# Attention with unnormalised probabilities: the reciprocal row sums multiply each unit's output on VectorE, spread over the partitions through DRAM

## The reference, cut to what matters

```python
scores = jnp.einsum('bqhgd,bkhd->bhgqk', q, k) * scale
bias = jnp.where(rel >= 0, -slopes * sqrt_dist, -jnp.inf)
attn = jax.nn.softmax(scores + bias[None], axis=-1)
out = jnp.einsum('bhgqk,bkhd->bqhgd', attn, v).reshape(B, S, NH * D)
return out @ w_o
```

## Time and profile before

| | |
|---|---|
| median of 3 runs | 2512.18 us (2511.98 to 2513.4) |
| time of the profiled execution | 2510.83 us |
| its span | 2508.5 us, mean granted clock 0.986 |
| PE busy | 2413.6 us (96%) |
| PEld busy | 2049.7 us (82%) |
| DVE busy | 1503.8 us (60%) |
| ACT busy | 1382.8 us (55%) |
| POOL busy | 779.4 us (31%) |
| DMA | 455.93 MB, mean 182 GB/s |
| chain that ended last | PE 87%, ACT 5%, DVE 4%, DMA 2% |

### The profile page before, as it was taken

The page is one execution under the profiler, slowest core; times in us unless marked ns, Lnnn a source line. Parts: engine busy times, 40 slices in busy tenths (PEclk is TensorE's granted clock), DMA queues, the critical chain, the costliest instruction groups (busy, mean ns, idle before and its releaser), DMA issues.

```text
span 2508.5 us, 35023 instructions
## 1 busy us (share of the span) xinstructions
PE 2413.6 (96%) x12128; PEld 2049.7 (82%) x12128; DVE 1503.8 (60%) x2817; ACT 1382.8 (55%) x3075; POOL 779.4 (31%) x1029
## 2 busy tenths in 40 slices
PE   5999999997899999999799999999999999999999
PEld 4787888886778888888688888888888888888887
DVE  6657455565755555545566666666656666666664
ACT  4432133334534123333777777777777777777764
POOL 3211000000320100000334535446345364454634
PEclk8999999998999999999999999999999999999999
DMA  4536344545345544543755565655656556555543
GB/s 148 189 132 213 134 161 158 201 174 218 115 135 185 176 151 168 201 169 141 279 193 188 184 214 182 219 175 182 220 188 218 185 183 212 195 201 201 185 168 126
DMA packets 118319, 455.93 MB, mean 182 GB/s; under 512 B 11945, under 2 KB 12089, under 8 KB 109184
## 3 DMA queue, kind: packets, MB, share of 16 engines
q1 hardware_dynamic: 86176, 334.37, 38.6%
q0 software_dynamic: 31968, 119.33, 13.7%
HBM read 276.96 MB, written 176.69 MB: 181 GB/s over the span
## 4 chain that ended last, share of the span: by engine, by line
PE 87%; ACT 5%; DVE 4%; DMA 2%; issue 1%; POOL 1%; SPq 0%; DVEq 0%; ACTq 0%; POOLq 0%
PE ps L637 27%; PE ps L639 27%; PE ps L638 27%; PE ps L824 5%; ACT wo L886 1%; ACT probs L1026 1%; DVE stats L1135 1%; ACT pt_hi L886 1%; DMA q<-qk_s 1%; ACT rows L915 1%; ACT probs L1040 1%; DVE w_lo L1121 0%; ACT res_hi L886 0%; DMA lora_lo<-lora_s 0%; DVE pt_lo L1121 0%
## 5 line engine op out<-in xcount | busy, mean ns | idle before, releaser
L886 ACT ACTIVATE w_hi<-raw 128x1024 fp32r<-128x1024 f32 x196 | 207.0, 1059 | 559.3 <-PE ps L639 440.3
L1121 DVE TENSOR_TENSOR w_lo<-raw,w_hi 128x1024 fp32r<-128x1024 f32 x196 | 239.1, 1224 | 357.8 <-ACT w_hi L886 357.6
L1389 DVE TENSOR_TENSOR acc<-ps,acc 128x512 f32<-128x512 f32 x448 | 298.3, 687 | 249.5 <-issue 225.1
L637 PE MATMUL ps<-x_hi,w_hi 128*128 128x512 f32 x1120 | 436.2, 389 | 0.0
L639 PE MATMUL ps<-x_hi,w_lo 128*128 128x512 f32 x1120 | 435.8, 389 | 0.0
L638 PE MATMUL ps<-x_lo,w_hi 128*128 128x512 f32 x1120 | 435.7, 389 | 0.0
L637 PE MATMUL ps<-wo,op_hi 128*128 128x512 f32 x896 | 365.5, 408 | 24.1 <-DVE wo L1121 24.1
L1026 ACT ACTIVATE probs<-probs,neg_max 128x512 f32<-128x512 f32 (+3 forms) x512 | 284.2, 567 | 172.2 <-DVE neg_max L1358 172.2
L639 PE MATMUL ps<-wo,op_lo 128*128 128x512 f32 x896 | 355.3, 397 | 0.0
L638 PE MATMUL ps<-wo,op_hi 128*128 128x512 f32 x896 | 354.4, 396 | 0.0
L1358 DVE CUSTOM_DVE_ANT_0 probs<-ps,bias 128x512 f32<-128x512 f32 (+3 forms) x512 | 220.7, 487 | 111.4 <-PE ps L639 107.5
(11 more groups left out here) (155 smaller groups left out, 4700.6 us busy)
## 6 DMA issues: line engine op xcount, KB each, us to landing
raw<-w_all SPq DMA_DIRECT2D x70, 1024.0 KB, 5.3
q<-qk_s SPq DMA_DIRECT2D x128, 512.0 KB, 3.9
acc<-acc_s SPq DMA_DIRECT2D x128, 512.0 KB, 5.2
acc_s<-acc SPq DMA_DIRECT2D x112, 512.0 KB, 7.8
qk_s<-res_hi POOLq DMA_DIRECT2D x40, 1024.0 KB, 4.6
qk_s<-res_a POOLq DMA_DIRECT2D x20, 1024.0 KB, 9.1
qk_s<-res_b POOLq DMA_DIRECT2D x20, 1024.0 KB, 5.2
k<-qk_s SPq DMA_DIRECT2D x32, 512.0 KB, 3.6
```

The source lines that it names most:

```text
L637: pe.matmul(to, st_hi, mv_hi, start=start, stop=False, skip_group_check=True)
L886: nc.scalar.activation(to, source, ACT.Copy).then_inc(signal, 1)
L1121: nc.vector.tensor_tensor(to, source, high.bitcast(F32), ALU.subtract).then_inc(signal, 1)
L1389: nc.vector.tensor_tensor(to, fill[f % 2][:, :], to, ALU.add).then_inc(s_acc, 1)
```

## The change

The four ACT instructions of `normalise` are gone and the transposes wait for the exponentials instead. ACT's copy `outputs` is gone; DVE now reads ps_o, multiplies by the reciprocal row sums and writes at_raw. There, the query rows lie along the free axis and are the same for all partitions, so a unit's 512 reciprocals have to stand in every partition: SP writes them to DRAM, waits for that DMA, and reads them back broadcast. In the tables, weight step 4 has its high part one place earlier, and its low part is made by POOL in four pieces instead of by DVE. Some small tensors are moved in SBUF to make room.

```diff
-HIGHS_FIRST = {10: (4, 6)}
-HIGHS_LAST = {8: (0, 1), 9: (3, 2), 10: (5,)}
+HIGHS_FIRST = {10: (6,)}
+HIGHS_LAST = {8: (0, 1), 9: (3, 2, 4), 10: (5,)}
 LOWS_EARLY = {9: (0,), 10: (2,)}
-LOWS_MIDDLE = {9: (1,), 10: (4,)}
-LOWS_LAST = {9: (3,), 10: (6, 5)}
+LOWS_MIDDLE = {9: (1,), 10: (6,)}
+LOWS_LAST = {9: (3,), 10: (5,)}
+BY_DVE = (0, 1, 3, 2, 6, 5)
+LOWS_POOL = {10: (4,)}
+BY_POOL = (4,)
...
+            def spread(n):                       # SP
+                if not 0 <= n < UNITS:
+                    return
+                sp.wait_ge(s_inv, n + 1)
+                if n >= 2:
+                    sp.wait_ge(s_at_raw, n - 1)
+                sp.dma_start(inv_s[n % 2].rearrange("(p i) -> p i", i=QT), row_inv[:, n % 2, :]).then_inc(s_inv_s, 16)
+                sp.wait_ge(s_inv_s, 16 * (n + 1))
+                if n == 0:
+                    sp.wait_ge(s_bank, 4 * TOTAL)
+                sp.dma_start(inv_all[n % 2][:, :], inv_s[n % 2].partition_broadcast(P)).then_inc(s_inv_all[n % 2], 16)
...
+                spread(n - 2)                    # SP loop: after the loads of q, k, v
                 out_weights(n)
                 sums_in_and_out(n)
...
+            def out_split(group, step):          # POOL, after out_low and wo_sums
+                pool.wait_ge(s_wo_hi, made(group, step))
+                for i in range(4):
+                    cut = slice(i * 256, (i + 1) * 256)
+                    last = nc.gpsimd.tensor_tensor(wo[:, step, 1, cut], wo_source(step)[:, cut],
+                                                   wo[:, step, 0, cut].bitcast(F32), ALU.subtract)
+                last.then_inc(s_wo_low, 1)
...
             def transposes(n):                   # PE
-                pe.wait_ge(s_probs, n + 1)
+                pe.wait_ge(s_exp, QT * (n + 1))
...
             def exponential(n, c):               # ACT
+                if n and c == 0:
+                    act.wait_ge(s_inv, n)
...
-            def outputs(n):                      # ACT
-                act.wait_ge(s_o, n + 1)
-                high(at_raw[s % 2][n % G // 2][:, n % 2, :], ps_o[:, :], s_at_raw)
-            def normalise(n):
-                act.wait_ge(s_inv, n + 1)
-                for i in range(QT):
-                    tile = probs[:, n % 2, OFF[i]:OFF[i] + (i + 1) * P]
-                    last = nc.scalar.activation(tile, tile, ACT.Copy, scale=row_inv[:, i:i + 1])
-                last.then_inc(s_probs, 1)
...
+            def outputs(n):                      # DVE
+                s = n // G
+                dve.wait_ge(s_o, n + 1)
+                dve.wait_ge(s_inv_all[n % 2], 16 * (n // 2 + 1))
+                if s >= 2:
+                    dve.wait_ge(s_op_lo, PARTS * (s - 1))
+                nc.vector.tensor_tensor(at_raw[s % 2][n % G // 2][:, n % 2, :].rearrange("p (i q) -> p i q", i=QT),
+                                        ps_o[:, :].rearrange("p (i q) -> p i q", i=QT),
+                                        inv_all[n % 2][:, :].rearrange("p (q i) -> p i q", i=QT),
+                                        ALU.mult).then_inc(s_at_raw, 1)
...
                 for part in making(n, LOWS_MIDDLE):
                     out_split(*part)
+                if 1 <= n <= UNITS:
+                    outputs(n - 1)
                 for f in todo[3:]:
                     add_fill(*f)
                 for part in making(n, LOWS_LAST):
```

More of the change, by code:

```diff
@@ L111, in block_program @@
         ident = at("ident", rest, [P, P])
[L112 to L124, removed]
+        slopes = at("slopes", rest + 512, [P, HEADS])
+        neg_max = at("neg_max", rest + 640, [P, QT])
+        row_sum = at("row_sum", rest + 672, [P, QT])
+        row_inv = at("row_inv", rest + 704, [P, 2, QT])
+        stats = at("stats", rest + 736, [P, 2, 2, 6])
+        moments = at("moments", rest + 864, [P, TT, 2])
+        rstd = at("rstd", rest + 928, [P, TT])
+        root = at("root", rest + 960, [P, TT])
+        newton = at("newton", rest + 992, [P, TT])
+        shift = at("shift", rest + 1024, [P, TT])
+        gbias = at("gbias", rest + 1056, [P, E])
+        gate_buf = at("gate_buf", rest + 1088, [P, 2, TT, E])
+        gate_col = at("gate_col", rest + 1344, [P, 10, TT])
         d_mask = at("d_mask", rest + 1664, [P, QT, R])
@@ L134, in block_program @@
         dist = at("dist", 32 * K, [P, SEQ])
+        inv_all = [at("inv_all0", 54 * K, [P, P * QT]), at("inv_all1", rest + 736, [P, P * QT])]
         bias = at("bias", 34 * K, [P, G, SEQ])
@@ L147, in block_program @@
         v_s = nc.dram_tensor("v_s", (BATCH, KV_HEADS, P, 2, QT, D), F32).ap()
+        inv_s = nc.dram_tensor("inv_s", (2, P * QT), F32).ap()
         acc_s = nc.dram_tensor("acc_s", (TOKENS, HIDDEN), F32).ap()
@@ L216, in block_program @@
         s_wo_lo = sem("s_wo_lo")
+        s_wo_low = sem("s_wo_low")
         s_bias = sem("s_bias")
@@ L221, in block_program @@
         s_inv = sem("s_inv")
-        s_probs = sem("s_probs")
+        s_inv_s = sem("s_inv_s")
+        s_inv_all = [sem(f"s_inv_all{i}") for i in range(2)]
         s_pt = sem("s_pt")
@@ L342, in made, with low_made @@
             return STEPS * group + WO_ORDER.index(step) + 1
+        def low_made(group, step):
+            if step in BY_POOL:
+                return s_wo_low, len(BY_POOL) * group + BY_POOL.index(step) + 1
+            return s_wo_lo, len(BY_DVE) * group + BY_DVE.index(step) + 1
         def used(group, step):
@@ L423, in out_weights @@
                 if n % GROUP_UNITS == 2 * G + 2 and group + 1 < GROUPS:
-                    sp.wait_ge(s_wo_lo, STEPS * (group + 1))
+                    sp.wait_ge(s_wo_lo, len(BY_DVE) * (group + 1))
+                    sp.wait_ge(s_wo_low, len(BY_POOL) * (group + 1))
                     sp.wait_ge(s_wo_sum, len(WO_SUMS) * (group + 1))
@@ L487, in _ @@
             for n in range(UNITS, UNITS + 3 * G):
+                spread(n - 2)
                 sums_in_and_out(n)
@@ L615, in wo_sums @@
                 if step == 5:
-                    pool.wait_ge(s_wo_lo, made(group, 1))
+                    pool.wait_ge(*low_made(group, 1))
                 for i in range(4):
@@ L631, in _ @@
                     wo_sums(group, step)
+                for group, step in making(n, LOWS_POOL):
+                    out_split(group, step)
         @block.tensor
@@ L844, in fill_in @@
                 if s % (SETS // GROUPS) == 0 and tile == 0:
-                    pe.wait_ge(s_wo_lo, made(s // (SETS // GROUPS), k))
+                    pe.wait_ge(*low_made(s // (SETS // GROUPS), k))
                 pe.wait_ge(s_op_lo, f + 1)
@@ L1092, in _ @@
                 s, _, new = shaped(n)
-                if 2 <= n < UNITS + 2:
-                    outputs(n - 2)
                 for part in making(n, HIGHS_FIRST):
@@ L1105, in _ @@
                     out_high(s, part)
-                if n < UNITS:
-                    normalise(n)
                 for part in making(n, HIGHS_LAST):
@@ L1367, in inverses @@
                 dve.wait_ge(s_exp, QT * (n + 1))
-                if n:
-                    dve.wait_ge(s_probs, n)
-                nc.vector.reciprocal(row_inv[:, :], row_sum[:, :]).then_inc(s_inv, 1)
+                if n >= 2:
+                    dve.wait_ge(s_inv_s, 16 * (n - 1))
+                nc.vector.reciprocal(row_inv[:, n % 2, :], row_sum[:, :]).then_inc(s_inv, 1)
+            def outputs(n):
[8 more added lines that the diff above has]
+                                        ALU.mult).then_inc(s_at_raw, 1)
             def transposed(n):
```

3 lines of the change are left out of this document (removed).

## The result

The changed kernel takes 2518.01 us (median of 10 runs, 2517.18 to 2522.12), the kernel before 2512.63 us beside it (10 runs, 2510.6 to 2517.64). The ratio is 1.0023, with a 95% interval of 1.0014 to 1.0033: **slower by 0.2%, where 2492 us and a gain were forecast.** The profiled execution took 2520.79 us with a span of 2518.6; before, these were 2510.83 and 2508.5. From the page of the kernel after: busy times, the shares of the chain, a costly group, two DMA issues.

What follows compares the result with a forecast made beforehand. TensorE's pace was taken as the bound, with one wait per group for VectorE's low part of weight step 2. Seven groups 18 us, first group 1, start 0: 19 to 20 us less, 2492 us; range 2480 to 2504.

Steps and rivals of the forecast that it cites:

- What bounds the kernel: Attention stage: TensorE at its pace, plus eight waits for VectorE's low part of weight step 2, 4.65 us each.
- ScalarE's part: Without normalise and outputs, ScalarE delivers high parts sooner and VectorE's 1.04 us of idle time before low(3) goes.
- The multiply: VectorE's new output operation, taken as 0.69 us; upper end 1.22 us, which would take 0.5 us from each group's gain.
- Low parts and GpSimd: VectorE's chain to low(2): low(3) 1.26 us, low(2) 1.22 us, so TensorE starts that step 1.3 us sooner.
- The clock: After TensorE's shortened gap of about 1.9 us, no fall of the clock: 1.38 us come back, 0.11 is paid.
- Rival 2: TensorE's clock still falls behind the shortened gap: 2502 us, or 2506 with a slow multiply as well; chance 0.15.
- Low(4) hidden: POOL makes this low part in 2.8 us, done by 1739.9, before TensorE needs it after 1740.4: no cost.
- SP's queue, steady: Write and broadcast of the reciprocals, 2.6 us each, about 6 us with issues: hidden, 5 us to spare.
- rival 4: The broadcast arrives late and VectorE waits every unit; a single late us costs 120, giving 2612 us; chance 0.05.
- The stage's start: First units of the attention stage: a gain of up to 5 us or a loss of up to 8, taken as 0.

Runs made afterwards that it cites:

- e7: Kernel before with one table edit: ScalarE makes the high parts of weight steps 4 and 6 after normalise, not before the first exponential; 2503.63 us.
- e8: Kernel before with high parts 4 and 6 after normalise, high(2) before high(3), low(3) after low(2), GpSimd's step 5 sum earlier; 2492.93 us.
- e3: The change, with VectorE's multiply reading the reciprocals in order instead of with a stride of four (outputs wrong); 2518.64 us.
- e9: The change from unit 7 on, earlier units as before, with a multiply without stride (outputs wrong) and GpSimd's step 5 sum earlier; 2503.16 us.
- e2: The change from unit 7 on; units 0 to 6 normalised and copied by ScalarE as in the kernel before; 2505.50 us.
- e6: The change from unit 7 on, with VectorE making low(2) before low(3) and GpSimd's sum for step 5 earlier; 2503.05 us.
- e1: The change, but the broadcast reads 512 values of x and SP does not wait for the small write (outputs wrong); 2505.42 us.
- e5: The change, with both small DMAs, write and broadcast, issued from ScalarE's queue instead of SP's; 2515.32 us.

## Why the prediction was wrong

**What bounds the kernel: right.** TensorE at its pace, with one wait per group for low(2); e7 and e8 only shortened that wait, and with it the falls of the clock, and took 8 and 20 us.

**ScalarE's part: right.** The idle times of VectorE in place 9 and before pt_lo are gone. But the freed ScalarE was needed for one thing only, not to stand before place 10's first exponential, and e7 has that from a table.

**The multiply: mis-sized.** The prediction took 0.69 us, the value of the nearest row, with 1.22 as the upper end. It measured 1.07, and 0.69 without the stride (e3). The Trainium skill (SBUF — State Buffer, Door 1) had spoken for a penalty, and the trace agrees with it: 0.38 us for 512 elements.

**Low parts and GpSimd: left out.** The prediction let VectorE's operations keep their lengths while moving them to where GpSimd is busy: low(2) went from 1.22 to 1.45 us. And it looked at ScalarE, VectorE and TensorE for the end of the wait, not at GpSimd's sum for step 5, which ended 0.3 us before low(2) began (e3 shows that it binds as soon as VectorE is sooner). With 2.36 us instead of about 1.9, the gain in the gap was 0.75 us a group and not 1.32.

**The clock: the step "I take no fall of the clock" failed in four groups of seven.** The one row on which it rested, the 2.33 us gap with 1.00 behind it, was no rule: the same gap gave both. At the 1.9 us that the prediction had in mind it was not tested; behind the seven gaps of 1.7 us in e9 the clock held. Rival 2 had the falls, at 2502 to 2506, and e2, the change without its start, took 2505.5: so the steady part alone would have missed the range too. Had the clock held in all, a group would have lasted 158.3 us and the seven gained 13.7; the falls took 6.4 of these, and the new waits for acc and, probably, what the start's 4.17 us gap left behind took the other 2.5.

**Low(4) hidden: right, with its own length mis-sized.** It took 3.80 us and not 2.8, and ended at 1597.9, 2.5 us ahead of the first matmul of k=4 at 1600.42. The cover was wide enough for the 1.0 us that was missing, and in e6, with a gap of 1.42 us, it still was. In e9, where more of GpSimd's operations had grown, it was not, and cost 1.35 us a group.

**SP's queue, steady: right in its result and wrong in its terms.** The write landed after 5.1 us and the broadcast after 4.5, where I took 2.6 each: about 10 us with the issues, of the 10.9 that the sum allowed. The ground, "512 KB loads that go first have landed when the sums are ready", failed: SP is itself late by its wait, so the load goes out only 1 us ahead of the write. Where k and v go with it, the broadcast comes late, as rival 4 had it, and TensorE loses some 1 to 2 us in the whole stage by it.

**The stage's start: the step that failed most.** "A gain of up to 5 us, or a loss of up to 8 (...): I take 0." It lost 12.8 us. The prediction had seen that the write queues behind a load of 14.54 us and that SP stands still, and then halved that and spread it over the units. But each of the first units waits for it anew: sums, write, broadcast, multiply, transposes is a chain, and the loads of the next unit hang on it too. Four such writes on one chain is what the trace shows, and e1 and e2 give 12.5 us back. It is the mechanism of rival 4, at a place where no output parts cover it; the prediction had put that rival's price on every unit and none on the start. It also had no term for the clock there, whose lower level is 5.0 of the 12.8 us.

What stays open: why the clock fell behind some gaps of 2.36 us and not behind others, which no run varied alone; and how the start's loss divides between SP's standing still and the write's landing.

## What to carry to other kernels

Here a round trip through DRAM was priced by what was under way when it started, not by its bytes; and in the first iterations of a pipelined stage, where nothing covers it, every repetition counts in full, so work these out one by one. Where an engine looks late, first try to reorder its queue before moving its work: one edit of two table lines gave 8 us and a new order on VectorE, GpSimd and ScalarE 12 more, where moving the work gave 5 and cost 13. When a wait is shortened, follow every producer behind it, also the ones that end just before the present last one: here GpSimd's sum stopped the gain in e3, and GpSimd's low(4) became the next wait in e9.

## What the runs showed of the hardware that was not expected

- A 2 KB write of 128 pieces of 16 bytes landed in 2.7 us (median) in e1, where a 512 KB load was issued some 5 us ahead of it, and in 5.1 in the change, where it was 1 us. At the stage's start, beside several such loads, it took up to 9.1 us from SP's queue and up to 8.1 from ScalarE's (e5).
- An fp32 operand with a stride of four elements made a 128x512 multiply 1.07 us instead of 0.69.
- VectorE's 1024-element low part, whose two inputs are both in SBUF, took 1.22 us alone and 1.3 to 1.8 beside GpSimd, and GpSimd's four pieces took 3.80 instead of 2.8, a single one 1.73 instead of 0.73 (e9); the multiply, with one input in PSUM, stayed at 1.05 to 1.10. The Trainium skill (SBUF — State Buffer, Who interferes with whom) names just this pair of cases; it says that the later of the two blocks fully. The stretches here agree with that: VectorE lost 0.1 to 0.6 us, no more than one of GpSimd's pieces of 0.7, and GpSimd lost 1.0 us, no more than one of VectorE's operations of 1.2.
- TensorE's clock fell behind all seven gaps of 3.11 us in the kernel before, behind four of the seven of 2.36 us in the change and five of the seven in e7, and behind none of the seven of 1.7 us in e9 or of 1.44 us in e8. Behind the gap of 2.77 us at e7's first place 10 it held.
